# The first cross-attention of an eight-block kernel: queries, value pieces, division, mask table and turn copies moved between slots and engines

## What is computed

```python
q = (queries @ wq.T + bq).reshape(b, s, h, dh)
k = (patch_representations @ wk.T + bk).reshape(b, p, h, dh)
v = (patch_representations @ wv.T + bv).reshape(b, p, h, dh)
scores = jnp.einsum('bqhd,bkhd->bhqk', q, k) * scale
patch_idx = jnp.cumsum(patch_boundaries, axis=1)
mask = jnp.arange(p)[None, None, :] > patch_idx[:, :, None]
scores = jnp.where(mask[:, None, :, :], jnp.finfo(scores.dtype).min, scores)
attn = jax.nn.softmax(scores, axis=-1)
out = jnp.einsum('bhqk,bkhd->bqhd', attn, v).reshape(b, s, d)
return out @ wo.T + bo
```

## Time and profile before

| | us |
|---|---|
| median of three executions (3453.9 to 3457.77) | 3457.45 |
| profiled execution, its own time | 3449.82 |
| its span | 3448.0 |
| first scores of the first attention to its last addition, in the trace | 42.7 to 460.9 |

### The profile page before, as it was taken

The page is one execution under the profiler, slowest core; times in us unless marked ns, Lnnn a source line. Parts: engine busy times, 40 slices in busy tenths (PEclk is TensorE's granted clock), DMA queues, the critical chain, the costliest instruction groups (busy, mean ns, idle before and its releaser), DMA issues. The chain is left out here.

```text
span 3448.0 us, 60530 instructions
## 1 busy us (share of the span) xinstructions
PE 3129.1 (91%) x22046; PEld 2635.4 (76%) x22046; DVE 1672.1 (48%) x3487; ACT 1563.6 (45%) x4177; POOL 1312.9 (38%) x1417
## 2 busy tenths in 40 slices
PE   5988868998989859899999999598999999997999
PEld 4777758996756559778888887488788888876998
DVE  3777760003566557544444444300444444445766
ACT  2555523443345435445555555244455555552332
POOL 0000001112100022157777766311577777774342
PEclk8999969999999959999999999699999999997999
DMA  5655535552100044200000000454000000001333
GB/s 140 137 131 132 131 124 201 184 182 73 50 1 1 3 145 148 80 13 15 15 16 15 16 13 1 155 211 147 20 13 13 13 13 13 12 1 43 120 107 92
DMA packets 146135, 253.21 MB, mean 73 GB/s; under 512 B 46892, under 2 KB 122664, under 8 KB 133304
## 3 DMA queue, kind: packets, MB, share of 16 engines
q1 hardware_dynamic: 132216, 223.65, 21.5%
q0 software_dynamic: 8064, 20.20, 2.1%
q10 hardware_dynamic: 5568, 5.51, 0.5%
HBM read 214.83 MB, written 34.46 MB: 72 GB/s over the span
## 5 line engine op out<-in xcount | busy, mean ns | idle before, releaser
L718 POOL TENSOR_SCALAR L_probs<-L_probs,L_inverse 112x375 f32<-112x375 f32 x512 | 651.0, 1271 | 119.3 <-issue 119.3
L866 DVE TENSOR_REDUCE L_negmax<-bank 112x1 f32<-112x375 f32 x768 | 395.0, 542 | 427.9 <-PE bank L470 357.1
L674 ACT ACTIVATE L_probs<-bank,L_negmax 112x375 f32<-112x375 f32 x768 | 435.2, 572 | 215.7 <-DVE L_negmax L866 210.6
L497 PE MATMUL bank<-ident,L_probs 112*125 112x112 f32 x2304 | 399.0, 282 | 19.3 <-POOL L_probs L718 12.3
L497 PEld LDWEIGHTS bank<-ident,L_probs 112*125 112x125 f32 x2304 | 337.9, 189 | 91.1 <-issue 50.7
L716 POOL TENSOR_TENSOR L_inverse<-L_sums,neg_one 112x1 f32<-112x1 f32 x512 | 296.3, 579 | 143.5 <-ACT L_probs L674 143.1
L654 ACT ACTIVATE L_probsT<-bank 125x336 f32<-125x336 f32 x512 | 231.9, 453 | 248.4 <-PE bank L497 248.4
L636 ACT ACTIVATE v<-bank 125x512 f32<-125x512 f32 x192 | 114.8, 598 | 266.7 <-PE bank L423 266.7
L704 POOL TENSOR_TENSOR L_stats<-L_stats,neg_half 112x1 f32<-112x1 f32 x48 | 26.9, 561 | 520.7 <-DVE L_stats L783 520.7
L512 PE MATMUL bank<-L_probsT,v 125*64 125x112 f32 x3072 | 207.0, 270 | 1.7 <-ACT L_probsT L654 1.1
L416 PE MATMUL bank<-L_ctx_hi,L_wk_hi 128*128 128x376 f32 x512 | 149.5, 373 | 30.2 <-DVE L_ctx_lo L850 22.6
(11 more groups left out here) (324 smaller groups left out, 7172.2 us busy)
## 6 DMA issues: line engine op xcount, KB each, us to landing
L0t_w<-in_F_w SPq DMA_DIRECT2D x35, 1024.0 KB, 4.8
L_keys<-spread_k SPq DMA_DIRECT2D x64, 376.0 KB, 6.4
L2t_w<-in_F_w SPq DMA_DIRECT2D x21, 1024.0 KB, 4.8
L_ctxT<-in_ctxT SPq DMA_DIRECT2D x48, 375.0 KB
w_all<-in_F_w SPq DMA_DIRECT2D x16, 1024.0 KB, 13.7
cap_w<-in_F_w SPq DMA_DIRECT2D x16, 1024.0 KB, 5.1
L3d_row<-comb_rows SPq DMA_DIRECT2D x64, 224.0 KB, 3.2
L_q<-spread_q SPq DMA_DIRECT2D x128, 56.0 KB, 2.2
```

Source lines behind the costliest of these rows:

```text
L497: ins = pe.transpose(psT[h % len(psT)][0:SJ, j * T:(j + 1) * T], probs[h % NB][:, j * SJ:(j + 1) * SJ], core.ident[0:T, 0:T])
L674: act.activation(probs[e % NB][:, :], psS[e % 2][0:T, 0:S], ACT.Exp, bias=negmax[b.par][:, e:e + 1], accum_out=sums[b.par][:, e:e + 1]).th ...
L718: pool.tensor_scalar(probs[h % NB][:, :], probs[h % NB][:, :], inverse[b.par][:, h:h + 1], None, ALU.mult)\
L866: dve.tensor_reduce(negmax[b.par][:, h:h + 1], psS[h % 2][0:T, 0:S], AX, ALU.max, negate=True).then_inc(maxed.sem, 1)
```

## The change

In the narrow attention alone: Q0 goes from slot 4 to 5, and DVE takes it in slot 6 instead of at once; V0, V1 and V2 go from slots 11, 13 and 15 to 2, 6 and 12; O0 goes from 7 to 8, Y0 from 9 to 10; the division goes from slot 6 to 7 and the mask table to 9. The turn copies of heads 1, 3, 5 and 7 are made by ACT, in slots 3, 5, 7 and 9, behind the exponential of that slot, and counted by a semaphore of their own, `probsT_act`. Which earlier piece each piece waits for is now worked out from one list of all pieces.

```diff
-        order = {0: ["K0"], 1: ["K1"], 3: ["L0", "L1"], 4: ["Q0"], 7: ["O0"], 9: ["Y0"], 11: ["V0"],
-                 13: ["V1"], 15: ["V2"]}
+        order = {0: ["K0"], 1: ["K1"], 2: ["V0"], 3: ["L0", "L1"], 5: ["Q0"], 6: ["V1"], 8: ["O0"], 10: ["Y0"],
+                 12: ["V2"]}
...
+    BY_ACT = () if wide else (1, 3, 5, 7)
+
+    def copies(b, h, by_act):
+
+        n = len([i for i in range(h) if (i in BY_ACT) == by_act])
+        return b.n * (len(BY_ACT) if by_act else H - len(BY_ACT)) + n
...
+        def sequence():
+
+            out = [(("first", 0, p), p, 0) for p in first_pieces if not own_bank(p)]
+            for n in range(B):
+                for h in range(H):
+                    out += [(("heads", n, p), p, n + d) for p, d in pieces_at(h, n == 0, n == B - 1) if not own_bank(p)]
+            return out + [(("tail", B - 1, p), p, B - 1) for p in every if p[0] in "OY"]
+
+        in_order = sequence()
+        prior_of = {key: in_order[i - 2][1:] for i, (key, _, _) in enumerate(in_order) if i >= 2}
...
-                        pe.wait_ge(probsT_ready.sem, probsT_ready.at(H * b.n + h - 1))
+                        if h < 2:
+                            pe.wait_ge(probsT_ready.sem, probsT_ready.at(copies(b, 0, False) + h - 1))
+                        elif h - 2 in BY_ACT:
+                            pe.wait_ge(probsT_act.sem, probsT_act.at(copies(b, h - 1, True)))
+                        else:
+                            pe.wait_ge(probsT_ready.sem, probsT_ready.at(copies(b, h - 1, False)))
...
-                    pe.wait_ge(probsT_ready.sem, probsT_ready.at(H * b.n + h + 4))
+                    pe.wait_ge(probsT_ready.sem, probsT_ready.at(copies(b, h + 4, False)))
+                    if h < 8:
+                        pe.wait_ge(probsT_act.sem, probsT_act.at(copies(b, h + 4, True)))
...
                             act.activation(probs[e % NB][:, :], psS[e % 2][0:T, 0:S],
                                            ACT.Exp, bias=negmax[b.par][:, e:e + 1],
                                            accum_out=sums[b.par][:, e:e + 1]).then_inc(exped.sem, 1)
+                        if not wide and h >= lag and h - lag in BY_ACT:
+                            take_probsT(b, h - lag)
...
-                        if not wide and not (b_first and h < lag):
+                        if not wide and not (b_first and h < lag) and before(b, h, lag)[1] not in BY_ACT:
                             take_probsT(*before(b, h, lag))
                         if h == 0 and not b_last:
                             normalise_start(b + 1)
-                        if h == (4 if wide else 6) and not b_first:
+                        if not wide and not b_last and h == 6:
+                            take("Q0", b + 1, where["Q0"][0])
+                        if h == (4 if wide else 7) and not b_first:
                             divide(b + -1, NG - 1)
                         if h == 2 and not b_last:
                             normalise_end(b + 1)
-                        if h == 6 and mask and not b_last:
+                        if h == 9 and mask and not b_last:
                             bar(b + 1)
```

More of the change, by code:

```diff
@@ L222, in cross_attention @@
         probsT_ready = core.counter("probsT_ready")
+        probsT_act = core.counter("probsT_act")
         pv_done = core.counter("pv_done")
@@ L289, in first_slots, with prior_to @@
             return out
+        def sequence():
[6 more added lines that the diff above has]
+        prior_of = {key: in_order[i - 2][1:] for i, (key, _, _) in enumerate(in_order) if i >= 2}
+        def prior_to(part, b, p):
+            prior, n = prior_of[part, b.n, p]
+            return prior, Batch(0, n)
         def last_slots():
@@ L554, in heads @@
                             at, (prior, pd) = where[p] if not b_last else last_where[p]
-                            piece(p, b + d, (at, (prior, b + pd)))
+                            prior = (prior, b + pd) if own_bank(p) else prior_to("heads", b, p)
+                            piece(p, b + d, (at, prior))
                 def first(b):
@@ L587, in tail @@
                     for p in [p for p in every if p[0] in "OY"]:
-                        at, (prior, d) = where[p]
-                        piece(p, b, (at, (prior, b + d)))
+                        piece(p, b, (where[p][0], prior_to("tail", b, p)))
                 closing = [p for p in every if not own_bank(p)][-2:]
@@ L655, in take_probsT @@
                                    psT[h % len(psT)][0:SJ, 0:J * T].rearrange("p (j t) -> p j t", t=T), ACT.Copy)\
-                        .then_inc(probsT_ready.sem, 1)
+                        .then_inc((probsT_ready if wide else probsT_act).sem, 1)
                 def take_raw(b):
@@ L921, in heads @@
                         for p, d in pieces_at(h, b_first, b_last):
-                            take(p, b + d, where[p][0] if not b_last else tails.index(p) % 2)
+                            if wide or p != "Q0":
+                                take(p, b + d, where[p][0] if not b_last else tails.index(p) % 2)
                         if wide and not b_last:
@@ L1014, in cross_attention @@
             s.stage_over(B)
-        for s in (scored, maxed, exped, turned, probsT_ready):
+        for s in (scored, maxed, exped, turned):
             s.stage_over(B * H)
+        probsT_ready.stage_over(B * (H - len(BY_ACT)))
+        probsT_act.stage_over(B * len(BY_ACT))
         pv_done.stage_over(B * H // 2 if wide else B * H // 4)
@@ L3095 @@
            + ["qkv_made", "rope_done", "barred_ready", "added", "x_biased", "wk_here", "x_first", "x_rest", "w_high", "relu_weights", "self_weights", "wide_weights", "w_split", "ctx_split", "k_high", "q_split", "weighed",
-              "raw_ready", "o_turned", "v_zeroed", "k_stored", "q_stored", "keys_here", "q_here",
+              "raw_ready", "o_turned", "v_zeroed", "k_stored", "q_stored", "keys_here", "q_here", "probsT_act",
               "comb_out", "w2_split", "w2_high", "small_here", "row_here0", "row_here1", "row_here2", "row_here3"])
```

## The result

| | before | after |
|---|---|---|
| median of 20 executions each, side by side | 3450.66 us (3445.53 to 3458.44) | 3461.73 us (3451.5 to 3467.06) |
| profiled execution's span | 3448.0 | 3460.3 |

The ratio is 1.0028, with a 95% interval of 1.002 to 1.0036: slower, by a little more than the 0.2% that was named as the limit of no change. The predicted 3460 us looks close, but part of that is luck. The three executions behind 3457.45 lay high; over 20 the kernel before takes 3450.66. By the prediction's own sum (+2.7) the new kernel would have come to 3453.4. It came to 3461.73. The direction was right; the size, +11.1 us, was four times the sum.

A forecast was written before the change was run, and what follows sets the result against it. The prediction took a chain of key and query transfers to bound each batch, not PE, DVE or ACT. All terms were 0 except +2.7 us for the clock; against 3457.45 it gave 3460 us, range 3447 to 3475.

The forecast's parts named there:

- The chain bounds the stage: At batch boundaries: slot 0 waits for the query loads, so transfers end the batch, which still takes 25 us or more.
- The key part stays at 5.67: Slot 0 to key store: nothing is put into slots 0 and 1, so 5.67 us stays, cost 0.
- Queries a slot behind cost 0: Query store issued 4.4 us after the key loads instead of 1.85, chain no longer; at worst 36 us.
- Context load 0: SP's context load goes out earlier, behind the last query load, and could delay its landing; cost taken as 0.
- PE ready 0.7 earlier: End of slot 15: PE through at 24.2 instead of 24.9, all of it wait; bounds 0.5 later, 2.8 earlier.
- The last batch 0, at most 0.5 either way: Last batch, without that wait or V, K, Q pieces: DVE loses four copies, ACT gains them; taken as 0.
- What the clock costs: Longer slot 0 waits drop PE's clock in the key part: two more falls at 1.34 us each, +2.7 us.
- The base: Starting time to which the sum was added: 3457.45 us, the median of three executions of the kernel before.
- Rival C: ACT's copies hold the turns in slots 5, 7 and 9, so PE comes late and ends the batch; 3474, chance 0.05.
- A: Rival: PE ready 1.5 us earlier or more, clock falls at every batch boundary; 16 us, about 3473, chance 0.14.
- B: Rival: the late queries lengthen the transfer chain, up to 2.6 us a batch; 3493, a third gives 3469; chance 0.07.
- D: Rival: a gain comes through because PE ends the batch, 10 us, 3447, or the chain gains 2; chance 0.14.

The follow-up runs named there:

- a_spq: The changed kernel with the query store issued ahead of the key loads in the SP queue; ratio 1.0125 against the kernel before.
- values_actq: The kernel before with only the value pieces moved (slots 2, 6, 12) and query stores issued from ScalarE's queue in slot 7; ratio 1.0013.
- b_actq: The kernel before with the query stores issued from ScalarE's queue in slot 7, key and query loads still from SP; ratio 0.9998.
- a_actcopies: The kernel before with only the turn copies of heads 1, 3, 5 and 7 moved to ScalarE; ratio 0.9995.

## Where the prediction was right and where not

- **The chain bounds the stage.** Right. All 15 waits of slot 0 end with the query loads, and a batch takes 26.25 us in the mean (24.7 to 29.2).
- **The key part stays at 5.67.** Right: 5.67 or 5.68 at all nine boundaries of the 14 that had no fall.
- **Queries a slot behind cost 0.** Right for the changed kernel: 14.07 against 14.04 from key store to query load. The store was issued 3.87 after the key loads (forecast 4.4) and the split came at slot 0 + 13.1 (forecast 13.6). a_spq showed what covered it, and the cost when the cover was gone.
- **Context load 0.** Right as far as can be seen: from query load to slot 0 it took 5.94 against 5.87, a mean that varies from 5.3 to 6.7 between boundaries in both.
- **PE ready 0.7 earlier.** Right: 0.58 (23.9 against 24.5, counted to where the weight loads go idle; the prediction's 24.2 and 24.9 are ends of the last matmul), and slot 10 waits 0.62 for ScalarE's copy where the walk gave 0.6. DVE's busy time in a batch fell by 1.6 (2 forecast) and ScalarE's rose by 1.2 (1.8 forecast), in stretches of a batch.
- **The last batch 0, at most 0.5 either way.** Wrong: +2.6. Some 1.7 is a fall, after the wait of 2.09 at 437.31, and 0.9 has no cause shown. I had counted falls for the 14 batches with a key part and forgotten that the last one, which has no chain to hide behind, pays for its fall in full.
- **What the clock costs.** The mechanism was right, the size was not, and this is the step that failed: "it decides at a quiet boundary's wait of about 2.2", and "two of the three: 2 x 1.34 = 2.7 us". The price of one was about right (1.33 to 1.36 at four of the five, 2.54 at 279.55, where the low clock held on into the K1 piece). But I took the 15 waits of one execution, added 0.7 to each, and compared them with a limit read from one fall. Waits do not recur at the same batch: the long ones were at 72.40, 303.70 and 407.78 before, and at 69.83, 148.12, 202.25, 279.55 and 308.75 after. And there is no sharp limit: between waits of 1.56 and 2.74 us both outcomes are on record. Three extra falls and one in the last batch made +5.0 and +1.7 instead of +2.7.
- **The base.** The sum was put on 3457.45, from three executions, though the profiled one (3449.82) lay 7.6 below it. The 20 executions have 3450.66, next to the profiled one. That error of +6.8 hid most of the missing +8.4.
- **Smaller slips.** The 0.88 of queue time for a value piece is not in the earlier trace rows, where 0.88 is an idle time of DVE; the trace has it elsewhere (a piece at 221.69, the next matmul at 222.57). The batch is 24.96 by the rows, not 24.97. Rival C adds its 14 us to 3460, which holds 2.7 for falls that its missing waits would not bring.

Of the rivals, A (the clock falls at every boundary) was nearest in kind, with falls at 6 of 15 boundaries, not all. Put on the better base, its 12 x 1.34 = 16 us gives 3467 and the forecast's 2.7 gives 3453.4; 3461.73 lies between, nearer to A. B, C and D did not happen.

## What to carry to other kernels

Where a chain of transfers sets the length of a loop, making the other engines faster buys nothing and may cost: the longer wait can drop TensorE's clock, and the drop lands on the part of the loop that heads the chain. Shorten the chain first, here by issuing a small store ahead of the large loads that would bury it, and make sure that what feeds the new head of the chain isn't the step that an earlier change made late. When a cost comes from an event that happens at some boundaries only, take its rate from all boundaries and its base from more than three executions.

## What was not expected of the hardware

Over the 14 profiles, at the boundaries behind the first where the query loads ended the wait:

| wait at slot 0, us | clock fell | of |
|---|---|---|
| under 1.5 | 0 | 65 |
| 1.5 to 2 | 8 | 45 |
| 2 to 2.5 | 17 | 25 |
| 2.5 to 2.9 | 10 | 11 |
| 2.9 and over | 41 | 41 |

The least wait with a fall behind it was 1.56 (284.18 in values_actq), the greatest without one 2.74 (305.03 in b_actq). A fall cost 1.33 us at the least, up to 1.67 in 49 of the 76, and 2.7 at the most. The Trainium skill, "TensorE: Matmul & The Clock Gate", section "HAM oscillation — how this bites in real kernels", tells of waits for transfers after which each tile starts on the lower clock; the trace agrees at 76 of these 187 boundaries. What decides in between stays open, and so does why the four falls inside batches of a_actcopies came after waits under 0.8 us.

A store of 112 KB issued behind 1.5 MB of loads landed near their end whether it was in their queue (7.7 us after issue) or in another engine's, issued later (4.9 us); issued ahead of them it took 1.8 us.
